# A filtered layer as one program: merged row stores, first rows and products loaded early, the way back by images

## What is computed

```
def filtered(x, h0, numerators, denumerator):
    a, b = pad(denumerator), pad(numerators)
    h = irfft2(rfft2(b) / rfft2(a))
    H = h0 + rfft2(h, s=(2 * l1, 2 * l2))[0]
    X = rfft2(x, s=(2 * l1, 2 * l2))
    Y = einsum('...hwi,ijhw->...hwj', X, H)
    return irfft2(Y)[..., :l1, :l2, :]

x = x + filtered(_gn(x), ...)      # layer 0
x = x + patch_mixer(_gn(x), ...)
x = x + conv3x3(_gn(x), ...)
x = x + filtered(_gn(x), ...)      # layer 1, called 3 in the inputs
```

## Time and profile before

| | |
|---|---|
| runs | 3528.9, 3530.05 and 3532.25 us, median 3530.05 |
| span of the profiled execution | 3535.8 us; the page gives no other time for it |
| mean granted TensorE clock | 0.968 of full speed |
| busy share of PE / PEld / DVE / ACT / POOL | 92 / 76 / 44 / 48 / 36% |
| DMA | 429.4 MB, mean 121 GB/s |
| layer 0: spectrum / convolve / back to image | about 638 to 705 / 707 to 1124 / 1127 to 1178 us |
| layer 1: the same | about 2996 to 3059 / 3061 to 3477 / 3480 to 3536 us |

### The profile page before, as it was taken

How to read it: one execution, slowest core, us unless ns; L and a number is a source line. 1 busy time by engine, 2 the same in 40 slices (tenths; PEclk the granted TensorE clock), 3 DMA queues, 4 the chain that set the end, 5 groups by cost and what they waited for, 6 DMA issues and landing times. The chain is left out here.

```text
span 3535.8 us, 82659 instructions
## 1 busy us (share of the span) xinstructions
PE 3239.9 (92%) x37272; PEld 2671.5 (76%) x37272; DVE 1570.7 (44%) x1926; ACT 1681.8 (48%) x1763; POOL 1257.6 (36%) x1018
## 2 busy tenths in 40 slices
PE   7999999589998699999899999999989978799996
PEld 6999998289997576666687776666678754499996
DVE  6788876411111434444765543343764454311111
ACT  3666665356553344444554434444454431455650
POOL 6888885055552102222540001222280000255550
PEclk9999999799999899999999999999999988899998
DMA  0333333877775521222133332121222353867765
GB/s 18 115 120 121 121 115 132 223 210 198 195 191 126 147 95 61 82 72 82 61 108 100 109 113 76 67 95 48 86 81 60 95 157 55 200 193 193 196 184 154
DMA packets 259193, 429.38 MB, mean 121 GB/s; under 512 B 27479, under 2 KB 105817, under 8 KB 257369
## 3 DMA queue, kind: packets, MB, share of 16 engines
q1 hardware_dynamic: 244746, 398.80, 38.8%
q10 hardware_dynamic: 14096, 25.31, 2.2%
HBM read 306.59 MB, written 114.29 MB: 119 GB/s over the span
## 5 line engine op out<-in xcount | busy, mean ns | idle before, releaser
L138 PE MATMUL m_bank<-xn,w 128*128 128x512 f32 x1536 | 618.3, 403 | 31.9 <-DVE m_store L1563 11.7
L139 PE MATMUL m_bank<-xn,w 128*128 128x512 f32 x1536 | 602.5, 392 | 0.0
L140 PE MATMUL m_bank<-xn,w 128*128 128x512 f32 x1536 | 601.9, 392 | 0.0
L802 PE MATMUL c_acc<-c_shifted,filt 128*32 128x224 f32 (+8 forms) x11264 | 455.4, 316 | 30.9 <-DMA c_shifted<-spectrum_dram 27.7
L802 PEld LDWEIGHTS c_acc<-c_shifted,filt 128*32 128x32 f32 x11264 | 441.8, 159 | 38.7 <-DMA c_shifted<-spectrum_dram 29.3
L581 ACT ACTIVATE filt<-filt 64x2048 f32<-64x2048 f32 (+3 forms) x256 | 424.7, 1758 | 20.4 <-PEq L18 11.0
L568 POOL TENSOR_TENSOR filt<-filt 64x1408 f32<-64x1408 f32 x64 | 259.5, 4055 | 486.8 <-DMA filt<-filters_dram 486.8
L129 ACT ACTIVATE w<-raw_weights 128x2048 fp32r<-128x2048 f32 x96 | 372.9, 3884 | 102.8 <-PE m_bank L140 101.5
L138 PEld LDWEIGHTS m_bank<-xn,w 128*128 128x128 f32 x1536 | 290.9, 189 | 173.1 <-issue 76.4
L133 DVE TENSOR_TENSOR w<-raw_weights,w 128x2048 fp32r<-128x2048 f32 x86 | 333.3, 3875 | 159.2 <-ACT w L129 159.2
L140 PEld LDWEIGHTS m_bank<-xn,w 128*128 128x128 f32 x1536 | 290.8, 189 | 62.9
(11 more groups left out here) (179 smaller groups left out, 6766.6 us busy)
## 6 DMA issues: line engine op xcount, KB each, us to landing
c_shifted<-spectrum_dram SPq DMA_DIRECT2D x256, 270.0 KB, 3.9
filters_dram<-f_stage SPq DMA_DIRECT2D x128, 512.0 KB, 3.5
filt<-filters_dram SPq DMA_DIRECT2D x240, 256.0 KB, 4.6
raw_weights<-in_L_conv_Wq SPq DMA_DIRECT2D x16, 2048.0 KB, 8.6
raw_weights<-in_L_conv_Wk SPq DMA_DIRECT2D x16, 2048.0 KB, 8.5
raw_weights<-in_L_conv_Wv SPq DMA_DIRECT2D x16, 2048.0 KB, 8.6
m_qf<-in_L_conv_Wout SPq DMA_DIRECT2D x128, 256.0 KB, 3.8
spectrum_dram<-s_rows SPq DMA_DIRECT2D x128, 136.0 KB, 2.4
```

What stands on the lines that cost most here:

```text
L138: pe.matmul(out, w[0], x[0], start=first, stop=False)
L139: pe.matmul(out, w[0], x[1], start=False, stop=False)
L140: return pe.matmul(out, w[1], x[0], start=False, stop=last)
L802: mm = nc.tensor.matmul(acc[k % 2][phase][32 * s:32 * s + 32, 0:B, LAGS * kb:HALF], filt[:, k, phase, :, :, 4 * kb + s].rearrange("p j c - ...
```

## The change

The three programs become one, `filtered_layer` (L585 of the changed kernel), with one set of tiles and one barrier.

- `rows`, the four slots, now lie in the place of group 3's rows (`shifted[:, 3]`), `cols` lies in `spare`, and the products that the way back reads (`prod`) lie over the filters of groups 0 to 2 of the ring. PSUM banks are shared by all stages.
- The row blocks come in another order: all even ones with an odd one after each third, and the other 11 odd ones at the end. A block is stored by one transfer of 128 partitions. After block 26 SP loads the rows of group 0, after block 31 those of group 1, and when all are stored it goes on with groups 2 and 3 as before.
- The products of the even frequencies are loaded from DRAM when groups 28 and 29 end, those of the odd ones up to group 27 when groups 29 and 30 end. Groups 28 to 31 are not stored in DRAM: two transfers each (L713 of the changed kernel) move their products from `out` to `prod` inside SBUF.
- The way back goes through the images outermost and the quarters innermost. PE makes the even halves of the first three units after group 31, and waits for the rest of the products before the odd halves.

```diff
+def filtered_layer(nc, layer, image, source, spare, filt, scratch, const, out_dram, tag):
...
+    UNITS = [(quarter, b) for b in range(B) for quarter in range(QUARTERS)]
+    AHEAD = 3
+    for i in range(C):
+        ROW_ORDER.append((0, i))
+        if i % 3 == 2:
+            ROW_ORDER.append((1, i // 3))
+    ROW_ORDER += [(1, i) for i in range(C // 3, C)]
+    LAST_EVEN = max(v for v, (par, i) in enumerate(ROW_ORDER) if par == 0)
+    FIRST_LOAD_AT = LAST_EVEN + 6
...
+        def row_block(i, par):
+            at = scratch["spectrum"][:, i, par * FW:(par + 1) * FW]
+            return bass.AP(tensor=at.tensor, offset=at.offset, ap=[[C * L * B * ROW, 2], [B * ROW, FW], [1, B * ROW]])
...
-            for u in range(2 * C):
-                i, par = u // 2, u % 2
-                sp.wait_ge(rows_ready, u + 1)
-                for part in range(2):
-                    sp.dma_start(scratch["spectrum"][part, i, par * FW:(par + 1) * FW],
-                                 rows[part * FW:(part + 1) * FW, u % 4].rearrange("p b q t -> p (b q t)")).then_inc(stored[u % 4], 16)
+            for v, (par, i) in enumerate(ROW_ORDER):
+                sp.wait_ge(rows_ready, v + 1)
+                sp.dma_start(row_block(i, par), rows[:, v % 4].rearrange("p b q t -> p (b q t)")).then_inc(rows_stored[v % 4], 16)
+                if v == FIRST_LOAD_AT:
+                    for k in range(4):
+                        sp.wait_ge(rows_stored[k], 16 * len(range(k, LAST_EVEN + 1, 4)))
+                    for s in range(4):
+                        load_rows(sp, 0, 0, s)
+            for s in range(4):
+                load_rows(sp, 1, 1, s)
             for k in range(4):
-                sp.wait_ge(stored[k], 16 * 2 * (2 * C // 4))
+                sp.wait_ge(rows_stored[k], 16 * (2 * C // 4))
...
+            def load_products(par, freqs, channels, signal):
+                for c in range(2):
+                    sp.dma_start(prod[FW * c + freqs.start:FW * c + freqs.stop, par, channels],
+                                 scratch["products"][FW * par + freqs.start:FW * par + freqs.stop, channels, c]).then_inc(signal, 16)
+
+            def move_products(g):
+                k, f = g % RING, 4 * (g - GROUPS // 2)
+                for c in range(2):
+                    sp.dma_start(prod[FW * c + f:FW * c + f + 4, 1],
+                                 out[c:128:2, k].rearrange("p b t q -> p (b t q)")).then_inc(last_in, 16)
...
+            sp.wait_ge(progress, POINTS * (LAST_BATCH + 1))
...
+            load_products(0, slice(0, FW), slice(0, 12), even_in)
+            sp.wait_ge(progress, POINTS * (LAST_BATCH + 2))
+            load_products(0, slice(0, FW), slice(12, 16), even_in)
+            load_products(1, SETTLED, slice(0, 8), odd_in)
+            sp.wait_ge(progress, POINTS * (LAST_BATCH + 3))
+            load_products(1, SETTLED, slice(8, 16), odd_in)
+            for k in range(RING):
+                sp.wait_ge(acc_out, LAST_BATCH + k + 1)
+                move_products(LAST_BATCH + k)
...
+            pe.wait_ge(even_in, 16 * 4)
+            pe.wait_ge(acc_out, GROUPS - 1)
+            for u in range(AHEAD):
+                back(u, 0)
+            pe.wait_ge(odd_in, 16 * 4)
+            pe.wait_ge(last_in, 16 * 2 * RING)
+            for u in range(AHEAD):
+                back(u, 1)
...
-                    act.wait_ge(added, 4 * (QUARTERS - 1) + b + 1)
+                    act.wait_ge(added, QUARTERS * (b + 1))
```

More of the change, by code:

```diff
@@ L591, in spectrum @@
         fwd_w = sb("fwd_w", [L, 2, 128])
+        inv_w = sb("inv_w", [128, 2, L])
         eps = sb("eps", [128, 1])
@@ new lines, in _ @@
+            for k in range(4):
+                sp.wait_ge(rows_stored[k], 16 * (2 * C // 4))
+            for m in range(8):
+                if m:
+                    sp.wait_ge(progress, SPREAD[m])
+                piece(sp, 2, 2, m)
+                piece(sp, 3, 3, m)
+            for n in range(1, N_BATCHES):
+                for k in range(RING):
+                    for m in range(8):
+                        sp.wait_ge(progress, POINTS * (RING * (n - 1) + k + 1) + SPREAD[m])
+                        piece(sp, RING * n + k, k, m)
@@ new lines, in _, with sum_of_filters @@
+        @block.gpsimd
+        def _(pool):
+            def sum_of_filters(n, k):
+                pool.wait_ge(filt_in[k], 64 * (n + 1))
+                sum_filters(nc.gpsimd, filt, k).then_inc(filt_summed, 1)
+            for k in range(EARLY):
+                sum_of_filters(0, k)
+            pool.wait_ge(freq_ready, 2 * C)
+            for n in range(N_BATCHES):
+                for k in range(RING):
+                    if RING * n + k >= EARLY:
+                        sum_of_filters(n, k)
+                    pool.wait_ge(rows_in[k], 64 * (n + 1))
+                    at = shifted[:, k].rearrange("p s b q t -> p (s b) q t")
+                    nc.gpsimd.tensor_tensor(total[:, k], at[:, :, 0, 0:HALF], at[:, :, 1, 0:HALF], ALU.add).then_inc(rows_summed, 1)
@@ L693, in _ @@
             nc.scalar.activation(std[:], var[:], ACT.Sqrt, bias=eps[:, 0:1]).then_inc(std_ready, 1)
[L694 to L701 removed]
+            for v in range(2 * C):
+                act.wait_ge(freq_ready, v + 1)
+                if v >= 4:
+                    act.wait_ge(rows_stored[v % 4], 16 * (v // 4))
+                nc.scalar.activation(rows[:, v % 4, :, :, LAGS:], freq[v % 2].rearrange("p b (t q) -> p b q t", q=2), ACT.Copy).then_inc(rows_ready, 1)
+                if v in TURN_AT:
+                    phases, column = TURN_AT[v]
+                    if v == min(TURN_AT):
```

396 lines of the change are left out of this document (166 added, 230 removed).

## The result

The changed kernel takes **3822.1 us** (median of 4 runs, 3809.0 to 3834.4) where the one before takes 3531.2: a ratio of 1.080, 95% interval 1.074 to 1.086. First the page's part 1 and the row stores in part 6 of the changed kernel.

The account below looks back on a forecast made before the run. PE, busy 92% of the span, bounds the kernel, so only its standstills between programs can change. Heads +268, tails +18 and output store -2 sum to +284 us: span 3820, median about 3814, range 3740 to 3915.

Parts of the forecast that it names:

- The merged store runs on two engines: Row stores: the outermost count of two in the DRAM pattern 2x64x544 leaves each store to two engines.
- S: Time of one merged row store, taken as 6.0 us, with 5.4 and 9.7 as ends.
- the formula of the head: Layer head, first store to group 2: 32 S + 1.8 latency + 3.1 group 0 loads + 21.4; +134 us per layer, +268 in all.
- fit before: Layer head: groups 0 and 1 both run before group 2 can start, so they add nothing.
- The tail, +18: Layer ends: last group to last add takes 62 us against 51.75 and 54.5, +18 us in all.
- +2 us: Tail: product loads hidden under the last groups' work end about 2 us after the last group.
- 8 x 3.9 = 31: Tail: eight SBUF moves of groups 28 to 31 at 3.9 us each, the last landing at +33 us.
- of about 30 us between the first three half units and the rest: Sign at the layer ends: PE waits that long for the moves after its first three even halves.
- near idle for some 190 us per layer: Sign at the layer heads: PE hardly works while the row stores go out.
- The copies, the share and the start of group 2: Head signs: ACT copies every 5.4 to 7 us, DMA share about 2/16, group 2 some 218 us after the first store.
- Images outermost, -2: Output stores: spread out, only one of 1 MB follows the last add, saving 2 us.
- The rival with sixteen engines: Row stores dealt over all 16 engines, 0.7 us each: heads -21 us a layer, 3504 us in all; chance 0.13.

Follow-up runs that it names:

- four-block stores: Changed kernel, spectrum relaid with an unused row after every 32, row store written 4x32x544, row loads of 64 partitions: 3678.1 us, ratio 1.043.
- one_of_128: Changed kernel with the spectrum relaid so a row store is one 128x544 transfer, row loads split into two of 64 partitions: 3563.1 us, ratio 1.006.
- two_queues: two_halves with half the product loads after group 31's moves land, only group 31 moved, by eight single-partition moves on SP and ACT, six even halves ahead: ratio 0.992.
- two_halves: Changed kernel with each row block stored again in two stores of 64 partitions: 3562.6 us, ratio 1.006.

## Why the prediction was right

**The merged store runs on two engines.** This step held: share 0.13, 50 GB/s, and the two- and four-block stores differ by a factor of two. S measured 5.58 us, 25.0 GB/s an engine, between the image load's 25.9 and the 22.3 of the product stores that I chose; the 14.4 GB/s of today's row stores belongs to their two halves, as I had it: in one_of_128 the same bytes from 128 partitions go at 240/(16 x 0.65) = 23 GB/s an engine. With S = 5.58 the formula of the head gives 32 x 5.58 + 1.8 + 3.1 + 21.4 = 204.9; measured are 205.8 and 206.1. Its parts came out too: the wait for all stores ends 184.6 us after the first (183.5 by the formula), and the rows of group 2 land 20.7 us later. What it left out is that group 1 ends at the same time. I had it "fit before", but its rows landed only at 852.76, and PE needed 17 us for it, so group 2 could not have begun sooner even with its own rows in place. The heads were forecast at +268 with S = 6.0 and measured +243.5, the largest difference among the sum's three terms. In all it was +284 forecast and +273 measured on the span; the four runs lie at 3809, 3811, 3833 and 3834, so their median, 3822.1, is further from the profiled time than I had it.
The rule of the Trainium skill ("DMA: Bandwidth & Descriptors", section "Why a DMA increments its semaphore by 16 and not by 1"), the largest count up to 16 that divides both sides' slowest dimension, gives 2, 4 and 16 for the three forms, and the runs agree with each. The table "Rules for kernel authors" on the same page asks for one 128-partition transfer in place of two halves; one_of_128 agrees for the store itself (240 GB/s at a share of 0.65, against 216 at 0.95), but only because its DRAM side is one dimension. The merged store of the changed kernel, with two pieces in DRAM, takes 5.58 us where two halves took 1.3; there the measurement decides against the table.

**The tail, +18, was near the measured +30 by luck: two errors in it cancel.** "+2 us" for the product loads was the step that failed: I took the groups over them as undisturbed, and they lost 23 and 27 us. "8 x 3.9 = 31" for the moves was too dear: PE's wait was 12.6 and 10.9 us, and from the last group to the last add it was 43 instead of 62. A move in a row of moves took 131 kB / 46 GB/s = 2.8 us, and at 1271, when group 31 ended, 0.69 of their 1.05 MB were still to go. The first error is 50 us where I had 4, the second 34 us less than forecast over the two layers, both larger than that of the heads. Together the two make about +30 where I had +18. The wait "of about 30 us between the first three half units and the rest" was therefore wrong. The sign "near idle for some 190 us per layer" was wrong as well: PE was busy for 39.7 of the 100 us from 700 to 800. The copies, the share and the start of group 2 were right.
The Trainium skill's "Door 1: The DMA port swizzle" ("SBUF — State Buffer") puts partitions that are 64 apart on different ports. A group's two moves then write through one port each; the estimate from that page, 4.8 us a move, is then 2.4 us a move and 54 GB/s for the two at once. The trace's 46 GB/s is near it. The gain of two_queues, where both ports are written at a time, fits too, but it also issues sooner. No run here varied the partitions written, so the port itself isn't shown.

**Images outermost, -2:** measured -1.8.

**The rival with sixteen engines** would have been off too. Its -21 us at the head took groups 0 and 1 at 25 us together; in one_of_128, where the store is on all engines, the head won 10 to 13 us, in two_halves 3 to 4, and each form came out 0.6% slower than the kernel before, where I had 3504. At the end of each layer the cause is the failed step above. At the head, groups 0 and 1 were slower than the trace of before let me think (37 us in two_halves), with stops that no releaser explains. They end behind an instruction packet like those of the last groups, but pacing the loads there did nothing, so what makes the packets late isn't settled.

## What to carry to other kernels

Before two transfers are merged into one, look at the outermost count of the new pattern on both sides: it decides how many engines carry it, and one transfer on two engines took four times as long as two on sixteen. A change of the layout that makes it one dimension gets the merge without the loss, though here it won nothing over two halves (3563.1 against 3562.6 us). Work hidden under PE isn't free when it fills the queues: ask for it in parts, look for waits of PE without a releaser, and see whether each ends just behind a packet of the instruction queue.

## What was not expected of the hardware

- Loads hidden under matmuls stopped PE for 2.4 to 6.4 us at a time with no releaser; all nine of the last groups ended 1.2 to 1.7 us after a 16 KB packet of the instruction queue had landed, one of them with the DMA engines nearly empty. Eight parts instead of three cut the three groups from 58.6 to 42.5 us, none at all to 35.8.
- Moves into a few partitions ran at 46 GB/s on 3 engines (128 KB into four partitions) and at 47 on 13 (32 KB into one), and with loads behind two of them all sixteen engines were busy at 74 GB/s together.
- Eight single moves are in 11.1 us after the first is issued in one queue and 7.7 in two. Of the difference 2.2 us are their faster issue; the rest is open between the port and the queue.
